# Cross-attention with scores formed twice: a mask added on VectorE, a second set with keys on the partitions, zeroed on GpSimd

## What is computed

```python
qp = q @ Wq.T;  kv = latent_kv @ Wkv_expand.T;  k, v = jnp.split(kv, 2, axis=-1)
# 16 heads of 32 columns: qh, kh, vh
scores = jnp.einsum('bhqd,bhkd->bhqk', qh, kh) * inv_sqrt_d
scores = jnp.where(causal, scores, jnp.finfo(scores.dtype).min)   # causal: key <= query
attn = jax.nn.softmax(scores, axis=-1)
out = jnp.einsum('bhqk,bhkd->bqhd', attn, vh)          # then @ Wout.T
```

## Time and profile before

| | us |
|---|---|
| median of 3 runs | 2698.35 (2691.79 to 2704.05) |
| the profiled execution | 2698.37 |
| its span in the trace | 2696.6 |
| TensorE busy | 2500.0 (93%) |
| VectorE busy | 1791.3 (66%) |
| ScalarE busy | 1169.1 (43%) |
| GpSimd busy | 873.1 (32%) |

### The profile page before, as it was taken

The page is one execution under the profiler, slowest core; times in us unless marked ns, Lnnn a source line. Parts: engine busy times, 40 slices in busy tenths (PEclk is TensorE's granted clock), DMA queues, the critical chain, the costliest instruction groups (busy, mean ns, idle before and its releaser), DMA issues.

```text
span 2696.6 us, 46484 instructions
## 1 busy us (share of the span) xinstructions
PE 2500.0 (93%) x16390; PEld 1343.9 (50%) x16390; DVE 1791.3 (66%) x4037; ACT 1169.1 (43%) x2370; POOL 873.1 (32%) x801
## 2 busy tenths in 40 slices
PE   6999999999998999999768989989989989989998
PEld 3445454454544454444344454455455455455466
DVE  7789766777776777777475665665665665565554
ACT  4444444444444444444244534533543443543523
POOL 2333333333333333333123322422422422422413
PEclk9999999999999999999868999999999999999999
DMA  5677666776666677696420001001001001000000
GB/s 149 143 170 184 136 155 151 168 163 139 158 159 138 155 153 177 151 196 135 130 78 16 10 8 36 5 12 36 1 16 36 1 17 36 1 17 24 4 19 7
DMA packets 454606, 235.14 MB, mean 87 GB/s; under 512 B 388328, under 2 KB 391016, under 8 KB 454376
## 3 DMA queue, kind: packets, MB, share of 16 engines
q1 hardware_dynamic: 454376, 232.07, 36.5%
HBM read 78.66 MB, written 32.77 MB: 41 GB/s over the span
## 4 chain that ended last, share of the span: by engine, by line
PE 71%; DVE 13%; SPq 5%; issue 4%; DMA 3%; ACT 3%; POOL 2%; DVEq 0%; ACTq 0%; POOLq 0%
PE ps L1363 19%; PE ps L1364 19%; PE ps L1365 18%; DMA mem<-mem 3%; SPq L537 3%; DVE mem L1197 2%; PE ps L1496 2%; PE ps L1497 2%; PE ps L1498 2%; DVE mem L1201 2%; SPq L556 1%; PE ps L1506 1%; PE ps L1510 1%; PE ps L1508 1%; PE ps L1549 1%
## 5 line engine op out<-in xcount | busy, mean ns | idle before, releaser
L1363 PE MATMUL ps<-mem 128*128 128x512 f16 (+6 forms) x3924 | 1216.9, 329 | 93.7 <-DMA mem<-mem 39.1
L1364 PE MATMUL ps<-mem 128*128 128x512 f16 (+6 forms) x3924 | 1222.8, 328 | 0.0
L1365 PE MATMUL ps<-mem 128*128 128x512 f16 (+6 forms) x3924 | 1212.3, 327 | 0.0
L1363 PEld LDWEIGHTS ps<-mem 128*128 128x128 f16 (+3 forms) x3924 | 410.2, 105 | 420.4 <-issue 113.5
L1365 PEld LDWEIGHTS ps<-mem 128*128 128x128 f16 (+3 forms) x3924 | 411.1, 105 | 316.6 <-issue 17.1
L1364 PEld LDWEIGHTS ps<-mem 128*128 128x128 f16 (+3 forms) x3924 | 413.1, 105 | 303.5 <-issue 16.6
L697 POOL TENSOR_TENSOR mem<-mem 128x500 f32<-128x500 f32 (+1 forms) x231 | 270.4, 1170 | 359.3 <-ACT mem L928 198.9
L647 POOL TENSOR_TENSOR mem<-mem 128x8 f32<-128x8 f32 x100 | 163.7, 1637 | 541.8 <-DVE mem L1000 541.8
L1319 DVE TENSOR_TENSOR mem<-mem 128x500 f16<-128x500 f32 (+1 forms) x231 | 144.3, 648 | 189.9 <-ACT mem L910 186.2
L659 POOL TENSOR_TENSOR mem<-mem 100x400 f16<-100x400 f32 x128 | 162.2, 1267 | 187.7 <-ACT mem L799 187.7
L711 POOL TENSOR_TENSOR mem<-mem 100x400 f32<-100x400 f32 x128 | 107.9, 854 | 339.4 <-DVE mem L1211 339.4
(11 more groups left out here) (122 smaller groups left out, 3196.8 us busy)
## 6 DMA issues: line engine op xcount, KB each, us to landing
x<-mem SPq DMA_DIRECT2D x100, 256.0 KB, 3.0
mem<-x SPq DMA_DIRECT2D x75, 256.0 KB, 3.5
mem<-in_x SPq DMA_DIRECT2D x50, 256.0 KB, 3.7
mem<-x SPq DMA_DIRECT2D x12, 1000.0 KB
mem<-mem SPq DMA_DIRECT2D x32, 200.0 KB
out<-mem SPq DMA_DIRECT2D x6, 1000.0 KB
mem<-in_wq SPq DMA_DIRECT2D x4, 1024.0 KB, 5.7
mem<-in_wk SPq DMA_DIRECT2D x4, 1024.0 KB, 6.9
```

Of the source, the lines that this page charges most:

```text
L1363: pe.matmul(out_ap, ah, bh, start=(i == 0), stop=False)
L1364: pe.matmul(out_ap, ah, bl, start=False, stop=False)
L1365: mm = pe.matmul(out_ap, al, bh, start=False, stop=(i == len(pairs) - 1))
```

## The change

The scores of a batch are formed twice. The first time as before (queries on the partitions), but without the mask matmul: VectorE adds the bf16 mask into an SBUF buffer `masked` and takes the max from it. The 100 x 16 maxima are split into two bf16 parts, transposed by one matmul and copied to `mxT`. The second time keys are on the partitions (`ckT` stationary, `qpT` moving), and a matmul of a constant `minus`, -1 at the two rows of each head, by `mxT` subtracts the maxima. ScalarE takes the exponential out of PSUM straight into `cpT`, GpSimd zeroes the keys behind the query there with an affine_select, and TensorE mixes the values with the unnormalised exponentials (bank 6) and, with a constant of ones, forms the sums on the same 128 x 400 layout (bank 5). VectorE inverts the sums, all 128 x 400, and multiplies (`divide`); ScalarE and VectorE split the product `co`.

The transposes of the probabilities, their copies, GpSimd's products and the small sums and reciprocals go. The pieces are dealt out anew, four of them ahead of the first scores, and alternate between banks 7 and 4; the last tile's piece is waited for one step later. GpSimd writes the constants anew in each group, with memsets and eight chained affine_selects, and its group loop is written out instead of a hardware loop.

```diff
-        OUT_AT, OUT_AFTER = {}, (6, 6)
+        OUT_FIRST, OUT_AT, OUT_AFTER = 4, {}, {}
+        OUT_AT[GB] = [[6, 1, 2]] + [[4, 1, 2]] * (GB - 2) + [[4, 1, 0]]
+        OUT_AT[REST] = [[8, 2, 5]] + [[6, 1, 5]] * (REST - 2) + [[8, 2, 0]]
...
+        def out_bank(t):
+            return (7, 4)[t % 2]
... GpSimd
-                        pool.wait_ge(c["rden"], g * 4 * GB + 4 * b + i + 1)
-                        pool.tensor_tensor(cprobs[0:S, i, :, :], cprobs[0:S, i, :, :],
-                                           crden[0:S, i, :].unsqueeze(2).to_broadcast([S, HG, S]),
-                                           ALU.mult).then_inc(c["norm"], 1)
+                        pool.wait_ge(c["exp"], g * 4 * GB + 4 * b + i + 1)
+                        pool.affine_select(out=cpT[0:S, i, :, :], in_=cpT[0:S, i, :, :],
+                                           compare_op=ALU.is_ge, fill=0.0, base=0,
+                                           pattern=[[0, HG], [1, S]],
+                                           channel_multiplier=-1).then_inc(c["causal"], 1)
... ScalarE
+                for b in range(nb):
+                    if b:
+                        act.wait_ge(c["pv"], g * GB + b)
+                        take_o(b - 1)
+                    for i in range(4):
+                        act.wait_ge(c["st"], g * 4 * GB + 4 * b + i + 1)
+                        act.activation(cpT[0:S, i, :, :],
+                                       ps[0:S, i, 0:HG * S].rearrange("p (h t) -> p h t", h=HG),
+                                       ACT.Exp).then_inc(c["exp"], 1)
+                take_o(nb - 1)
... VectorE
+                def largest_scores(b, i):
+                    dve.wait_ge(c["sc"], n + 1)
+                    if b or i:
+                        dve.wait_ge(c["mx"], n)
+                    dve.tensor_tensor(masked[0:S, :, :], sc, mask[0:S, :, :],
+                                      ALU.add).then_inc(c["masked"], 1)
+                    dve.wait_ge(c["masked"], n + 1)
+                    dve.tensor_reduce(mxs[0:S, i, 0:HG], masked[0:S, :, :], AX.X,
+                                      ALU.max).then_inc(c["mx"], 1)
+                def divide(b):
+                    dve.wait_ge(c["pv"], g * GB + b + 1)
+                    dve.reciprocal(cden_r[:, :, :],
+                                   ps[:, 5, 0:KC * S].rearrange("p (c t) -> p c t", c=KC)
+                                   ).then_inc(c["rden"], 1)
+                    dve.tensor_tensor(co[:, :, :],
+                                      ps[:, 6, 0:KC * S].rearrange("p (c t) -> p c t", c=KC),
+                                      cden_r[:, :, :], ALU.mult).then_inc(c["co"], 1)
+                for b in range(nb):
+                    for i in range(4):
+                        largest_scores(b, i)
+                    split_largest(b)
+                    take_largest(b)
+                    if b:
+                        divide(b - 1)
+                    some_out(b)
                     if b:
                         take_o(b - 1)
... TensorE
+                def scores(b):
+                    for i in range(4):
+                        if b:
+                            pe.wait_ge(c["exp"], g * 4 * GB + 4 * (b - 1) + i + 1)
+                def shifted_scores(b):
+                    pe.wait_ge(c["mxe"], g * GB + b + 1)
+                    for m in range(KC):
+                        for i in range(4):
+                            pe.matmul(ps[0:S, i, m * S:(m + 1) * S],
+                                      ckT[r0:r0 + CD, m, b * S:(b + 1) * S],
+                                      qpT[r0:r0 + CD, m, b * S:(b + 1) * S],
+                                      start=True, stop=False)
+                        for i in range(4):
+                            mm = pe.matmul(ps[0:S, i, m * S:(m + 1) * S],
+                                           minus[r0:r0 + CD, m, :], mxT[r0:r0 + CD, :],
+                                           start=False, stop=True)
+                for b in range(nb):
+                    scores(b)
                     if b:
+                        mix(b - 1)
+                    some_out(OUT_AT[nb][b][0])
+                    largest(b)
+                    some_out(OUT_AT[nb][b][1])
+                    shifted_scores(b)
+                    some_out(OUT_AT[nb][b][2])
```

More of the change, by code:

```diff
@@ L707, in cross_attention @@
                 nt, tm = tiles_of(nb)
+                if not last_nb:
+                    pool.wait_ge(s["add"], ALL)
+                pool.memset(ones[0:S, :], 1.0).then_inc(c["const"], 1)
+                pool.memset(mxs[0:S, :, :], 0.0).then_inc(c["const"], 1)
+                pool.memset(minus[:, :, :], 0.0).then_inc(c["const"], 1)
+                for i in range(8):
+                    pool.wait_ge(c["const"], g * 11 + 3 + i)
+                    pool.affine_select(out=minus[:, :, :], in_=minus[:, :, :],
+                                       compare_op=ALU.not_equal, fill=-1.0,
+                                       base=-(i // 2 * CD + i % 2 * HG),
+                                       pattern=[[-1, HG], [0, S]],
+                                       channel_multiplier=1).then_inc(c["const"], 1)
                 for b in range(nb):
                     for i in range(4):
-                        pool.wait_ge(c["rden"], g * 4 * GB + 4 * b + i + 1)
-                        pool.tensor_tensor(cprobs[0:S, i, :, :], cprobs[0:S, i, :, :],
-                                           crden[0:S, i, :].unsqueeze(2).to_broadcast([S, HG, S]),
-                                           ALU.mult).then_inc(c["norm"], 1)
+                        pool.wait_ge(c["exp"], g * 4 * GB + 4 * b + i + 1)
[3 more added lines that the diff above has]
+                                           channel_multiplier=-1).then_inc(c["causal"], 1)
                 for t in range(nt):
@@ L723, in _ @@
             cross_attention(0, GB, 0)
-            over_groups(pool, layer)
+            for g in range(FULL):
+                layer(g, GB, GB if g < FULL - 1 else REST)
+            if REST:
+                layer(FULL, REST, 0)
         @block.scalar
@@ L865, in cross_attention, with take_o @@
                                    ).then_inc(c["qpe"], 1)
[L867 to L881, removed]
+                def take_o(b):
+                    act.wait_ge(c["co"], g * GB + b + 1)
+                    act.activation(coT_hi[:, :, b * S:(b + 1) * S], co[:, :, :],
+                                   ACT.Copy).then_inc(c["ohi"], 1)
+                for b in range(nb):
                     for n in (beside_first(b) if not last_nb else []):
@@ L1213, in add_residual, with take_o @@
+                def take_o(b):
+                    dve.wait_ge(c["ohi"], g * GB + b + 1)
+                    dve.tensor_tensor(coT_lo[:, :, b * S:(b + 1) * S], co[:, :, :],
+                                      coT_hi[:, :, b * S:(b + 1) * S],
+                                      ALU.subtract).then_inc(c["olo"], 1)
                 def add_residual(t):
@@ L1489, in project_out @@
                 if piece == 0:
+                    pe.wait_ge(c["dsum"], g + 1)
+                if piece == FC:
                     pe.wait_ge(c["dlo"], g + 1)
-                elif j == 0:
-                    pe.wait_ge(c["add"], g * NT + t)
+                if j == 0 and t >= 2:
+                    pe.wait_ge(c["add"], g * NT + t - 1)
                 h_hi, h_lo, w_hi, w_lo = ((hb_hi[:, j, a:b], hb_lo[:, j, a:b], wd_hi[:, j, :],
```

197 lines of the change are left out of this document (96 added, 101 removed).

## The result

The changed kernel takes 2795.51 us (median of 4 runs, 2789.27 to 2798.85) against 2696.93 for the kernel before beside it: a ratio of 1.036, 95% interval 1.033 to 1.039. The forecast was 2794. The profiled execution took 2789.27 us (span 2787.6), 90.9 more than the one of before; it is the fastest of the four, the others took 2792 to 2799.

A forecast was written before the change was run, and what follows sets the result against it. TensorE, busy 2500 of 2696.6 us, was taken as the bound, its new idle as the question. 2698 plus 81 (group 0 12, five groups 65, last group 4) plus 15 for the clock gave 2794 us; range 2735 to 2850.

The forecast's parts named there:

- The reciprocal: VectorE's 128x400 inversion: 2.6 us, delaying ScalarE's copy and so the next exponentials; 10.3 us of a group's 13.
- The chain: Dependent steps of a cross-attention batch: 10.75 us for the first, 12.85 with an earlier batch, against 9.23 before.
- The group: Five batches, from the end of query projections to the last feed-forward output piece: 85.35 us against 72.3.
- The clock: Half-clock work behind the batches' new idles of 2.8 us: 15 us in all, bounds 0 and 60.
- the third rival: Clock falls in the batches and stays low, 5.9 us more for 20 batches: 2910 us; chance 0.03.
- Group 0: First group, at half clock without pieces: four batches 55.8 us against 46.1; with the tail 12 us more.
- The five groups: Five-batch groups behind the first: 13 us more each, 65 us, with the clock's 15 us added separately.
- The last group: Group of two batches, with more pieces and one reciprocal on each side: 4 us more.
- The cheap reciprocal: VectorE's long reciprocal takes only 0.57 us: 2716 us in all; chance 0.09.
- The dear one: VectorE's reciprocal costs 8.3 ns an element, 3.5 us: 2830 us in all; chance 0.11.
- Mask add at half price: VectorE's mask add and max from SBUF take 0.3 us, with a cheap reciprocal: 2660 us; chance 0.03.
- Dearer zeroing: GpSimd's float32 zeroing is dearer than forecast; at 1.3 us each a batch is 1.5 longer: 2825 us; chance 0.02.

The follow-up runs named there:

- run 1: Changed kernel with ScalarE's copy of the divided output moved behind the next batch's exponentials, VectorE's remainder one batch later: 2739.33 us, ratio 1.013.
- run 2: Changed kernel with the 128x400 reciprocal replaced by a plain copy, so the output is multiplied by the sums: 2718.05 us, ratio 1.007.
- Run 6: Changed kernel with GpSimd's zeroing done twice on every quarter, the second waiting for the first: 2868.89 us, ratio 1.064.
- run 3: Changed kernel without VectorE's mask add, the max taken over all scores of a row: 2793.79 us, ratio 1.034.
- run 9: Kernel without mask add, copy moved, loop start placed, cross-attention's end rearranged; plus one max over four quarters and three pieces moved: 2657.37 us, ratio 0.985.
- run 5: Changed kernel with nine zero products filling TensorE's idles before the third to fifth batches' scores and the first projection: 2785.37 us, ratio 1.033.
- runs 3 and 4: The second of these: changed kernel with both ScalarE's copy behind the exponentials and no mask add on VectorE: 2719.97 us, ratio 1.007.
- the kernel with 128 memsets: Kernel without mask add and with the copy moved, plus 128 one-element memsets ahead of VectorE's loop (start 3003): 2718.39 us, ratio 1.007.

## Why the prediction was right

**The reciprocal.** 2.65 us measured, 2.6 forecast from readings of two and four elements: 6 ns an element carries over to 400. The estimate from the repeat count in the Trainium skill, "VectorE: DVE Perf Modes", section "First, the fixed hardware budget", was 3.3 us; this trace shows less, and the measurement decides. Runs 1 and 2 show that it costs where I put it, in ScalarE's copy ahead of the exponentials. Of the 10.3 us a group that I gave it, run 1 gives back some 8.5, by its batch spacing (4 times 2.1). Run 2, which takes away the wait at the group's end as well, gives back 10.5 to 12.6 from one group's first scores to the next, the clock's part included.

**The chain.** The first batch took 10.40 us (10.75), the later ones 12.60 to 12.70 (12.85). The add and the max are spaced 0.61 and 0.68 us, four quarters take 5.1 (5.2), each as forecast. What was a little off is the small bf16 products: the second scores with them took 1.1 us (1608.62 to 1609.7) where I had 1.39; at 0.05 us for four of them they lie at the low end of my 0.2 to 1.2.

**The group.** 85.8 us against 85.35, in part by luck: the four spacings of its batches sum to 0.9 us less than forecast, the stretch behind the fourth projection is 1.1 longer (11.1 against 9.95), because the turning of the last rows waits 1.13 us for VectorE's norm, a wait that my sum does not have. The later groups are 1.9 us longer, 87.7, through the clock.

**The clock.** I gave it 3 us a group. The first group's two dips had room behind VectorE's part, as reckoned (0.1 us in the spacing); from the next group on the batch of 13.1 us and the end show it. By that the clock costs 4 times 1.9, about 8 us, in the five groups, where my term was 15; the way it costs is the one forecast, an idle and then work at half clock that nothing covers, and its size was about half. Run 6 shows how near the third rival was: with 2.39 us of waiting before the value products the mean granted clock of a batch is 0.79.

**What cancelled.** By the start of the first scores of each group, the sum of 90.9 us parts (but for 0.3 us ahead of them) into 15.7 for group 0, 68.2 for the five others (13.6 each) and 7.3 for the last (the four pieces counted with the group in which they lie). Forecast were 12, 65 plus 15, and 4. Three terms were mis-sized:
- Group 0, +3.7: I had let its end cost almost nothing more. Its last batch and first projections stay at the lower clock until 18.1 us behind the start of the last scores (13.7 before), and the fourth projection waits 2.13 us, with a dip behind it.
- The five groups, -11.8 in sum. In the first of them the two dips of the batches cost nothing that the 85.8 us show, in the others 1.9 us, where I had 3: 5 us. The rest I had not looked for, since it lies outside the cross-attention. Four groups of before have an idle of 1.99 to 2.23 us in the next stage and some 3 us at half clock behind it. Their counterparts now are 1.90 to 1.93 us, with no dip behind them: 1.7 us back in each, 7 us.

```profile
1679.15 0.39 PE L1409 MATMUL ps<-mem 128*128 128x500 f16 x1 [1.90 <-DVE mem L1358]
```

- The last group, +3.3: its end has idles of 2.4, 1.7 and 3.9 us, the last before the projection that waits for the final reciprocal; I had counted the reciprocal there, not the lower clock behind the wait.

So the traces' difference is 90.9 where 96 was forecast: +7 and -12 partly cancelled. That the median came out within 2 us of the forecast is luck on top, since the profiled run is the fastest of four. The range of 2735 to 2850 was never in danger.

**Rivals.** The cheap reciprocal: ruled out by its row, and its price (2716) borne out by run 2. The dear one: ruled out by the row. The clock staying low: not in the changed kernel (0.91 in the middle window); run 6 comes nearer with 0.79 in a batch. Mask add at half price: 575 ns, ruled out. Dearer zeroing: 602 ns on average, but the median is 543, where I had 547 (six calls in group 0 take 0.7 to 2.6 us); nobody waits in the steady batches (three waits, 4.8 us in all). No change of pace: ruled out.

## What to carry to other kernels

Price an operation that the trace shows only in small by the spacing of the small ones, not by their duration, and then ask which engine, in its program order, stands behind it: the 2.65 us, against 0.57, cost 77 us (the changed kernel against run 2), and moving one copy took 56 of these away. Slack that is reckoned at full clock is gone when an idle brings the clock down, so a delay in a batch that idles already can cost more than its own length. And when an edit that must save time saves none, look for stalls that the profile gives no releaser for: where a loop starts in an engine's code was worth 28 to 30 us here.

## What the runs showed of the hardware

- VectorE's reciprocal of 128x400 from PSUM: 2650 ns, the same to 5 ns in 32 instances; a copy of the same tile 567 (run 2), a product of that size 576. A max over 100x1600 from PSUM took 2.61 us as four instructions (run 3) and 1.83 us as one (run 9).
- VectorE stalls of 3.2 to 3.8 us at the head of a loop, twice per pass in the four passes that are entered by the jump back, when the loop starts at instruction 2875 or 3003 of its code; none at 2895 or 2899, and none in the first pass.
- TensorE's granted clock ahead of the feed-forward stage: idles of 1.99, 2.01, 2.01 and 2.23 us had 3 us near 0.5 behind them, idles of 1.54, 1.46 and 1.90 to 1.93 us had none. Elsewhere, with other work ahead, idles of 2.45 us had a dip behind two of three in each group, and idles of 2.14 us before the fourth projection none, while in run 5 two of 2.13 us at the same place had one. So the length of an idle alone does not decide.
- A VectorE step of 125x32 took 3.62 us (else 0.19) beside GpSimd's 3.60-us move of 125x2048; in runs 3 and 4 and in the kernel with 128 memsets each stalled group has one step of 3.5 to 3.9 us there (else 0.19 or 0.42).
